# A two-pass routed FFN around an attention block: six pauses taken out of each sort, the first weights moved behind the first rows, filler matmuls in three waits, one small product moved

## The reference

```
x = x + 0.5 * ffn(layernorm(x))
x = x + attention(layernorm(x))          # 16 heads of 8, causal, 1024 keys
x = x + 0.5 * ffn(layernorm(x))          # the same weights as the first

def ffn(x):                              # 352 hidden units
    out = expert(x, shared)              # silu(x g) * (x u), then d
    w = weights of the top 2 of 7 routed experts, from softmax(x wr + rb)
    return out + sum of w[e] * expert(x, routed[e])
```

## Time and profile before

| | |
|---|---|
| median of 3 runs | 550.03 us |
| the three runs | 544.83, 550.03, 550.59 us |
| the profiled execution | 545.58 us |
| its span on the core | 543.8 us |
| granted TensorE clock, mean | 0.977 |
| busy: PE, DVE, ACT, POOL | 92%, 72%, 59%, 49% |

### The profile page before, as it was taken

One profiled execution on the slowest core, in us unless ns is written; L12 is line 12 of the kernel. 1 busy time (PEld: TensorE's weight loads), 2 busy tenths in 40 slices (PEclk: granted clock), 3 DMA queues, 4 the chain that ended last, 5 costly groups with the idle time before them and its releaser, 6 DMA issues.

```text
span 543.8 us, 12828 instructions
## 1 busy us (share of the span) xinstructions
PE 499.8 (92%) x4302; PEld 363.5 (67%) x4302; DVE 389.0 (72%) x1050; ACT 319.0 (59%) x691; POOL 265.8 (49%) x390
## 2 busy tenths in 40 slices
PE   4898989998898899999999999999898899899994
PEld 2788989998755554444444444446547799899994
DVE  4777845567479999898989798973566674454835
ACT  3464444457444577878786778677675344344632
POOL 6399988874484411222312121211348689854440
PEclk9899999999999999999999899989999999899998
DMA  8931424232743634050506050300001131433213
GB/s 271 312 91 49 116 65 119 78 113 79 225 158 93 206 81 164 21 178 8 184 1 184 2 184 3 107 1 4 2 10 36 45 81 52 130 85 94 83 40 116
DMA packets 35069, 52.63 MB, mean 97 GB/s; under 512 B 6016, under 2 KB 23936, under 8 KB 34368
## 3 DMA queue, kind: packets, MB, share of 16 engines
q1 hardware_dynamic: 27648, 39.03, 24.7%
q0 software_dynamic: 4480, 9.25, 5.2%
q10 hardware_dynamic: 2880, 3.55, 2.1%
HBM read 31.93 MB, written 28.00 MB: 110 GB/s over the span
## 4 chain that ended last, share of the span: by engine, by line
PE 44%; DVE 32%; POOL 13%; issue 5%; DMA 3%; ACT 2%; SPq 1%; DVEq 0%; POOLq 0%; ACTq 0%
DVE mxp L1923 24%; POOL z_rows L1264 9%; PE psum L974 8%; PE psum L1823 6%; PE psum L1782 5%; PE psum L957 4%; PE psum L935 4%; PE psum L937 4%; PE psum L936 4%; POOL idle L1276 3%; PE psum L1713 2%; PE psum L1723 2%; DMA wall_f<-in_ffn_sd 1%; PE psum L997 1%; PE psum L1612 1%
## 5 line engine op out<-in xcount | busy, mean ns | idle before, releaser
L1923 DVE TENSOR_REDUCE mxp<-psum 128x1 f32<-128x512 f32 (+3 forms) x320 | 179.4, 628 | 17.9 <-PE psum L1723 14.2
L1979 ACT ACTIVATE probs<-psum 128x512 f32<-128x512 f32 x256 | 136.6, 600 | 36.1 <-PE psum L1782 34.9
L1048 ACT ACTIVATE silu<-psum 128x352 f32<-128x352 f32 x107 | 49.6, 464 | 98.6 <-PE psum L937 98.6
L1093 DVE TENSOR_TENSOR act<-silu,psum 128x352 f32<-128x352 f32 x107 | 55.5, 519 | 64.3 <-ACT silu L1048 63.6
L1782 PE MATMUL psum<-queries,keys 32*128 32x512 f32 (+7 forms) x384 | 98.3, 419 | 1.2 <-ACT probs L1979 1.2
L1289 POOL DMA_INDIRECT y_rows<-ys,to_row x76 | 74.3, 977 | 50.8 <-DVE ys L1129 29.6
L974 PE MATMUL psum<-wall_f,at 128*128 (+1 forms) x648 | 90.8, 276 | 4.1 <-DVE x L1131 2.9
L2028 POOL TENSOR_SCALAR_AFFINE_SELECT probs<-probs 128x512 f32<-128x512 f32 x48 | 29.6, 639 | 124.0 <-ACT probs L1979 124.0
L974 PEld LDWEIGHTS psum<-wall_f,at 128*128 128x128 f32 x648 | 81.1, 192 | 5.2 <-ACT at L1056 3.4
L1782 PEld LDWEIGHTS psum<-queries,keys 32*128 32x128 f32 (+1 forms) x384 | 50.9, 187 | 34.6 <-ACT probs L1979 17.5
L1823 PE MATMUL psum<-probs,vg 128*32 128x512 f32 (+2 forms) x640 | 73.3, 534 | 0.0
(11 more groups left out here) (254 smaller groups left out, 848.7 us busy)
## 6 DMA issues: line engine op xcount, KB each, us to landing
z_rows<-q_stack SPq DMA_DIRECT2D x12, 682.5 KB, 5.5
keys<-k_stack SPq DMA_DIRECT2D x32, 128.0 KB, 5.4
queries<-q_stack SPq DMA_DIRECT2D x8, 512.0 KB, 5.0
zg_early<-z_rows SPq DMA_DIRECT2D x44, 65.0 KB, 2.0
yc<-y_rows SPq DMA_DIRECT2D x10, 256.0 KB, 3.3
zg_late<-z_rows SPq DMA_DIRECT2D x32, 65.0 KB, 2.0
yc<-y_rows ACTq DMA_DIRECT2D x6, 256.0 KB, 3.0
wall_f<-in_ffn_rd SPq DMA_DIRECT2D x1, 1344.0 KB, 16.5
```

Of the source, the lines that this page charges most:

```text
L1923: e.tensor_reduce(dst, scores, AX.X, ALU.max).then_inc(K.A["taken"], 1)
L1979: e.activation(strip_of(K, w)[:, j, :], slot(K, u, d, n)[:, 0:strip_width(w)], ACT.Exp, scale=SCALE).then_inc(K.A["ex"], 1)
```

## The change

In both passes no pause follows the scatters of the last three tiles of part 1 (six scatters, two experts each). At the start, ACT makes the high parts of the rows 0 and 1 ahead of both shared weights, and POOL the root of rows 2 ahead of the low parts of both. Busy matmuls are added in three places: one call at steps 9 and 11 of pass 0 (into the bank of the sorted rows), three ahead of the wait for tile `WHOLE` in pass 1, which had none. `n_mr` of the first 512 tokens moves from behind `mix` 1 to ahead of it, one step earlier.

```diff
-AWAKE = [{0: 2, 1: 1}, {}]
-ROWS_AWAKE = (2, 0)
+AWAKE = [{0: 2, 1: 1, 9: 1, 11: 1}, {}]
+ROWS_AWAKE = (2, 3)
...
             for _ in range(AWAKE[f].get(step, 0)):
-                busy_pe(K, bank(K, Y_BANK))
+                busy_pe(K, bank(K, Z_BANK if step > 1 else Y_BANK))
...
+CLOSE = TT - 3
...
     if (f, g) in NORM_FOR_PAUSE:
         norm_rstd_pool(K, f, NORM_FOR_PAUSE[f, g])
-    elif g % TT > 0:
+    elif 0 < t < CLOSE:
         pause_pool(K, f == 1 and t < HALF)
...
-... 43: (("n_stats", 0),), 44: (("mix", 1),), 45: (("n_mr", 0), ("n_stats", 1)),
+... 43: (("n_stats", 0),), 44: (("n_mr", 0), ("mix", 1)), 45: (("n_stats", 1),),
...
             router_weights_act(K)
-            weights_hi_act(K, 0)
             norm_hi_act(K, 0, 0)
             norm_hi_act(K, 0, 1)
-            weights_hi_act(K, 1)
+            for m in range(SHARED_WEIGHTS):
+                weights_hi_act(K, m)
...
             norm_rstd_pool(K, 0, 1)
-            weights_lo_pool(K, 0)
             norm_rstd_pool(K, 0, 2)
-            weights_lo_pool(K, 1)
+            for m in range(SHARED_WEIGHTS):
+                weights_lo_pool(K, m)
```

More of the change, by code:

```diff
@@ L2251 @@
              15: (("lists", (1, 0)),), 16: (("lists", (1, 1)),), 17: (("lists", (1, 2)),), 18: (("lists", (1, 3)),)}
-BEHIND_DVE = [{0: (("query", 0),), **{step: (("weights_lo", m),) for step, m in zip((3, 6, 12, 13), ROUTED_WEIGHTS)}, 19: (("small", 0),), 22: (("weights", 0),), 42: (("mix", 0),), 43: (("n_stats", 0),), 44: (("mix", 1),), 45: (("n_mr", 0), ("n_stats", 1)),
+BEHIND_DVE = [{0: (("query", 0),), **{step: (("weights_lo", m),) for step, m in zip((3, 6, 12, 13), ROUTED_WEIGHTS)}, 19: (("small", 0),), 22: (("weights", 0),), 42: (("mix", 0),), 43: (("n_stats", 0),), 44: (("n_mr", 0), ("mix", 1)), 45: (("n_stats", 1),),
                46: (("n_mr", 1), ("n_lo", 0)), 48: (("q_lo", 0), ("n_lo", 1)), 50: (("q_lo", 1),)},
```

## The result

The change made the kernel slower. Four executions took 558.35 to 565.99 us, median 562.42; the kernel before, run beside it, 544.83 to 550.59, median 550.26. The ratio is 1.024, with an interval of 1.019 to 1.029. The profiled execution took 558.35 us with a span of 556.6, 12.8 more than the one of before. The forecast was 546.5, its range ended at 550.5.

What follows compares the result with a forecast made beforehand. It read PE as holding 44% of the chain, DVE 32%, POOL 13%. Gains of 1.0 (pass 0 at `WHOLE`), 1.2 (product) and 1.3 (pass 1's filler), 3.5 us off the median, gave 546.5, range 540.5 to 550.5.

Steps and rivals of the forecast that it cites:

- The pauses: Part 1's scatters: each removed memset worth 0.31 us, last scatter 1.5 earlier; half of pass 0's 1.0 gain, 0 in pass 1.
- 1.0 us of further scatter time would be free: Pass 0 at tile `WHOLE`: PE's filler covers the rest of POOL's gain, so scatters could take 1.0 us more without loss.
- Scatters back to back get slow: Rival on part 1's unpaused scatters: each of the last five takes 1.92 us in place of 0.97; 554.9 us, chance 0.06.
- The product: `n_mr` ahead of `mix` 1 lets ACT's z run in idle time and ends PE's wait of 1.33: -1.2 us.
- The filler in pass 1: At tile `WHOLE`, six busy matmuls hold PE's clock, so the tile takes about 2.03 us in place of 3.34: -1.3 us.
- Steps 9 and 11: Pass 0: added busy matmuls fit into PE's waits of 1.04 and 0.71 us for DVE; counted as 0.
- The start: Row casts ahead of weights let the router begin at 15.4, when the last bias lands, in place of 15.97: 0.5 us.
- The sum without the pauses: Forecast gains left over: 0.5 from the start, 1.2 from the product, 1.3 from pass 1's filler, 3.0 us together.
- The two levels of the runs: Executions near 545 and 550 us, inferred to differ by slow-clock stretches in the attention; lower level as rival 542.1, chance 0.36.

Runs made afterwards that it cites:

- c0: The kernel before, unchanged, executed again to look at its trace once more; 550.75 us in one execution.
- e2: The kernel before with only the six pauses of each pass taken out; median 562.06 us, ratio 1.023 to the kernel before.
- f1: The kernel before with only the moved product and the three busy calls of pass 1; median 545.99 us, ratio 0.995.
- e1: The changed kernel with its pauses put back, all other parts kept; median 549.74 us, ratio 0.995 to the kernel before.
- g1: The kernel before with the last six pauses of each pass cut from 384 to 192 elements; median 557.69 us, ratio 1.012.
- p0: The kernel before with the pauses behind the last six scatters of part 0 out, part 1's kept; median 561.51 us, ratio 1.021.
- m3: The kernel before without memsets between part 1's last scatters, each waiting for DVE to take out one more tile; median 553.85 us, ratio 1.009.
- m2: The kernel before with two memsets behind each of the last six scatters of part 1; median 553.57 us, ratio 1.007.
- b1: e1 with a second memset behind each of the first ten result scatters of a pass; median 551.39 us, ratio 1.007 to the kernel before.
- q1: The kernel before with part 1's last six pauses moved behind the last scatter, six memsets in a row; median 555.35 us, ratio 1.008.

## Why the prediction was wrong, point by point

**The pauses: the step that failed.** Right was all that concerns POOL: 1.26 apart, 0.96 each, the last scatter 1.5 us earlier and another 1.4 by the start, the load 2.96 earlier. Wrong was the sentence that their removal is "worth 0.31", a gain with no price for anyone else, and with it "1.0 us of further scatter time would be free". I costed the pause as POOL's own idle time and never asked who uses it. PE's signals do. The price is 8 to 10 us in each pass against the first trace of before, and 6 to 9 against c0, which pays a part of it already (e2 in the columns "step 27" and "pass 1"); e2 shows it alone, and 2 pauses cost it as well as 6.

**The rivals.** "Scatters back to back get slow" had the right place and the right sign (554.9, at 0.06), but not the mechanism: none of the unpaused scatters was longer than 0.96, and in 72 to 76, where the loss arose, DVE did nothing. What I held against it, the two result scatters of the earlier trace rows, showed only that a scatter isn't lengthened; what others do beside it I hadn't read (in that trace nothing is late there, 0.36). The Trainium skill's rule on the shared port ("SBUF — State Buffer", the trap "DVE blocks DMA") led me to say that a pause neither helps nor harms without such DVE work. The rule is about POOL's writing, which was not slowed here; the conclusion that I drew from it is what e2 refutes.

**The product**: -1.2 forecast; in f1 -1.4 up to step 47 and -1.1 up to the attention's first row maxima (37.7 in place of 38.8 us from step 41), by the very times that the prediction gives. In the change and in e1 it was spent, since `mix` 0 came late there.

**The filler in pass 1**: the mechanism was right, the size holds for some executions alone. The tile took 1.98 in f1 and 1.98 after the change, forecast 2.03; the six busy matmuls took 1.46, counted as 1.55. But in c0, without filler and after a wait of 1.10, it took 2.02 (468.75 to 470.77): the clock had not fallen. So 1.3 is gained where it falls, and nothing where it doesn't.

**Steps 9 and 11**: PE's waits shrank from 1.04 and 0.72 to 0.59 and 0.26 in e1, and nothing behind them moved. Counted at 0, and so it is.

**The start**: the router waits for `b_p`, as said. Its landing is what varies: 10.0 to 11.9 us in the traces of before, c0, the change and e1. The router began at 14.53, 15.15, 15.19 and 16.38 in the four runs with the change (mean 15.3), at 15.64 to 16.33 in the others. That is 0.6 on the mean against 0.5, and less than nothing in a single execution.

**The sum without the pauses**: 0.5 + 1.2 + 1.3 = 3.0 forecast, e1 has 0.0054 x 550.2 = 3.0, with an interval from 0.2 to 5.7. That the two agree is luck: in e1's trace the product was spent and the router began at 16.38, later than before, and the medians differ by 0.5 only.

**The two levels of the runs.** The inference from the clock doesn't explain the two traces of before, which have two stretches each; there the lateness of PE's signals makes the 5 us. Across the kernels it holds: each stretch of the attention with the lower clock costs about 2.3 us: 209.8 without one, 212.2 with one, 214.5 with two, 216.9 with three; f1's two and the three of g1 and p0 cost less. They come and go between executions of any of these kernels.

**What stays open.** Shown is that the gap between POOL's scatters decides how late PE's signals arrive. Not shown is what the two share, why PE's are hit and ACT's and DVE's are not, and why some executions are free of it at the same gaps of 0.60: the first trace of before, and f1 in pass 0 (0.5 at most). Records of semaphore updates are missing from every trace but that first one; but f1 and b1, in time in pass 0, lack as many as c0, some 300 each, so missing records by themselves don't go with the lateness. All executions were recorded; whether the recording itself takes part was not tried.

## What to carry to other kernels

A pause that keeps an engine off the others' way has its users elsewhere: before taking one out, read in the trace what happens on the other engines while the paused engine is busy, and what happens at the end of the pause. When an engine seems to wait for one that has long been done, compare the producer's next instructions with the consumer's start, and look for a third engine whose rhythm the delay follows. And read two executions of the kernel before where its runs differ by as much as the effect in question: the one shown here was free of the very thing that the change made worse.

## What the runs showed of the hardware

PE's signals to ACT and DVE arrived up to 11.4 us late with or just behind indirect scatters that POOL issued with gaps of 0.30 us (p0), up to 5.2 with 0.44 (g1 in pass 1), up to 3.3 with 0.60 (e1 in pass 1, 2.2 in pass 0; at most 0.5 in pass 0 of f1), and in time with 1.00 to 1.07 (m3, m2, b1). Not each short gap did it: three result scatters 0.30 apart, the last at 479.39, left nothing late in the first trace. With the pauses in, signals came out 0.03 to 0.04 us after the end of a pause (e1, c0). Once they had piled up, scatters with gaps of 0.60 kept them back for 3 us (the change) to 10 us (p0) more, a stop of 2.8 us freed them in 1.5 (q1). The scatters' own landings were not affected: SP began the load 2.5 us after the last one was issued (71.68 to 74.19), with 7 unpaused in a row.
